# Stores of weight factors moved to GpSimd's queue, and the order of factor work on ScalarE and VectorE changed, in a fused gated cross-attention and FFN kernel

## The chip, the cores and the metric

The kernel runs on one core of a Trainium2 chip. The metric is the device time of one execution in microseconds, the median of three runs. Before the change it is 1135.29 us (1135.28 to 1135.34).

## The reference

```python
def attn(h, mem, mask):                       # h [32,128,512], mem [32,128,512]
    scores = einsum('bsd,bmd->bsm', h, mem) / sqrt(512)
    a = softmax(where(mask, scores, -1e30), -1)
    return where(any(mask), einsum('bsm,bmd->bsd', a, mem), 0)
def ffn(x, w_gate, w_up, w_down):             # 512 -> 2048 -> 512
    h = silu(x @ w_gate) * (x @ w_up)
    # of every 4 neighbours along the 2048 keep the 2 largest by magnitude
    return sparsify_2to4(h) @ w_down
x = x + tanh(g_xattn) * attn(layernorm(x), ctx, mask)
x = x + tanh(g_ffn)   * ffn(layernorm(x), w_gate, w_up, w_down)
```

There are 32 sequences of 128 rows, so 4096 rows of 512 go through the FFN. All is float32.

## The kernel before

**Two parts.** The first part, up to about 140 us, is the attention for the 32 sequences with the layernorms; it writes the sum so far to the output in HBM and keeps the transposed, normalised rows for the FFN. Then the FFN runs in 16 steps `s` (4 pairs of 512-row blocks times 4 quarters of the 2048 hidden columns), each of two units `u = 2s` and `2s + 1`.

**A unit on TensorE.** The gate and up products of a unit go by Strassen's scheme: seven products `k = 0..6`, each for two tiles `e`, each six matmuls, since a float32 value is split into a rounded high part and a low part (high times high, high times low, low times high). That makes 84 matmuls (`product`, lines 1218 to 1222). A product waits for its weight factor (`w_lo_done`, later `w_loaded`) and for PSUM to be free again: product 0 waits for `gated0` of the unit before (`h0_done`), product 2 for `copy_a0`, product 4 for `copy_a1`, product 5 for `copy_d0`. After a unit from the third on comes the down product of the step before, `down(s-1, order)` (lines 1289 to 1291): four tiles of 12 matmuls into two PSUM buffers `ps_y`, so tile `t` waits until ScalarE has copied tile `t-2` out (`copy_y`, line 704).

**Units 1 to 7 are built, 8 to 31 reloaded.** In steps 0 to 3 the seven weight factors of the next unit are made on the way: SyncE loads pieces of the raw weights (`load_w_piece`, line 252, buffer `w_raw`), ScalarE spreads them (`spread`, line 284) into `w_blk`, VectorE forms sums (`w_sum`, lines 306 to 317), ScalarE rounds the high parts (`w_high`, line 296) into `w_ring`, VectorE subtracts for the low parts (`w_low`, line 300), and SyncE stores each factor to HBM (`store_w`, line 391, 512 KB), from where later steps load it again (`load_w`, line 398). `spread` of piece 1 waits until `w_low` of factor 5 of the unit before has read the place.

**The rest of a unit.** ScalarE copies PSUM (`copy_a0`, `copy_a1`, `copy_d0`), applies silu, takes magnitudes (`absolute`, line 677), rounds the kept hidden values (`h_high`, line 684) and copies y out (`copy_y`). VectorE adds products (`add_c11`, `add_c22`, `add_c12`), multiplies gate by up (`gated0`, `gated1`, lines 955 and 961), compares magnitudes and counts (`compare`, `count_wins`), masks (`keep`, line 995) and makes low parts (`h_low`, `dn_low` for the down weights, line 1009). `x_high_at` and `x_low_at` with `x_sum` (lines 336, 341, 348 to 358) make the row factors for the next pair, one of 14 at a time; `x_stored_at` stores them.

**Order.** Each engine's instructions run in program order, which is written out by hand. SyncE's DMA queue is in order too: an issue behind a wait waits. GpSimd only does `add_y` (line 575) in the FFN: a DMA for each tile of y that adds it to the output in HBM. `y_out` has four buffers; `copy_y` waits for the addition of four tiles before.

## Time and profile before

| what | value |
|---|---|
| median of 3 runs | 1135.29 us |
| the profiled execution's own time | 1133.34 us |
| its span, first to last instruction | 1131.6 us |
| mean granted clock of TensorE | 0.992 |
| TensorE busy with matmuls | 1084.2 us, 96% |
| VectorE busy | 811.6 us, 72% |
| ScalarE busy | 621.2 us, 55% |
| GpSimd busy | 199.3 us, 18% |
| moved by DMA | 254.76 MB, mean 225 GB/s |

Times in rows are microseconds from the span's start. A row of the timeline is start, duration, engine, line, operation, output <- inputs, sizes, count, and in brackets how long the engine sat idle before it and who released it. Matmuls overlap: a row says 0.39 us, yet one starts every 0.227 us. A table of stretches gives, for each, its length, each engine's busy time with its count of instructions, the granted TensorE clock (1.00 is 2.4 GHz, 0.50 is 1.2 GHz), the DMA engines' mean busy share and GB/s.

### The profile page before, as it was taken

The page shows a single profiled execution, that of the slowest core. Times are in us where ns is not written, and L with a number is a line of the kernel's source. Part 1 is how long each engine was busy: PE and PEld are TensorE (multiplying, and loading weights), DVE is VectorE, ACT ScalarE, POOL GpSimd, SP SyncE. Part 2 cuts the span into 40 slices and gives each one's busy share as a digit, 9 for nine tenths or more (in the row PEclk, how much of TensorE's full clock was granted, in tenths as well). Part 3 has the DMA queues.
Part 4 walks back from the last instruction along what each step waited for, and adds up shares of the span by engine and source line. Part 5 has one row for each costly group of instructions (what it writes and reads, how often), then busy time and mean ns, then how long its engine had stood idle before and what let it go on. Part 6 is the DMA issues. An engine that isn't in the chain of part 4 may idle for free.

```text
span 1131.6 us, 15204 instructions
## 1 busy us (share of the span) xinstructions
PE 1084.2 (96%) x4960; PEld 881.5 (78%) x4960; DVE 811.6 (72%) x1421; ACT 621.2 (55%) x1132; POOL 199.3 (18%) x393
## 2 busy tenths in 40 slices
PE   6988898898998999999999999999999999999998
PEld 4767676686876888888888888888888888888886
DVE  6999869888696676657685757475756666575765
ACT  6989677566665454444454545455545444444552
POOL 5777400110001111111100101111111111111001
PEclk9999998999999999999999999999999999999999
DMA  7999685798887977787779777887878666767726
GB/s 267 326 336 320 216 314 194 204 262 273 271 236 219 371 219 193 191 239 216 190 228 347 211 203 204 215 250 190 227 219 282 159 152 154 197 149 199 195 32 136
DMA packets 92350, 254.76 MB, mean 225 GB/s; under 512 B 9072, under 2 KB 9072, under 8 KB 87920
## 3 DMA queue, kind: packets, MB, share of 16 engines
q1 hardware_dynamic: 74416, 221.28, 55.9%
q0 software_dynamic: 17856, 32.51, 21.1%
q8 instruction: 40, 0.66, 0.2%
q14 instruction: 38, 0.31, 0.1%
HBM read 154.14 MB, written 99.61 MB: 224 GB/s over the span
## 4 chain that ended last, share of the span: by engine, by line
PE 72%; DVE 18%; issue 4%; DMA 3%; ACT 2%; SPq 1%; DVEq 0%; POOL 0%; ACTq 0%
PE ps_a L1218 9%; PE ps_a L1220 9%; PE ps_a L1222 9%; PE ps_y L1289 9%; PE ps_y L1291 9%; PE ps_y L1290 9%; PE ps_d L1220 4%; PE ps_d L1222 4%; PE ps_d L1218 4%; PE ps_c L1218 2%; PE ps_c L1222 2%; PE ps_c L1220 2%; DVE bn L919 2%; DVE beats L969 2%; DVE bn L878 1%
## 5 line engine op out<-in xcount | busy, mean ns | idle before, releaser
L575 POOL DMA_DIRECT2D out_rows<-y_out x124 | 107.5, 868 | 874.8 <-ACT y_out L704 850.0
L1218 PE MATMUL ps_a<-xm,w_ring 128*128 128x512 f32 x512 | 201.1, 393 | 6.0 <-DVE hidden L955 3.6
L1289 PE MATMUL ps_y<-dn,h_hi 128*128 128x512 f32 x480 | 191.0, 398 | 14.0 <-ACT y_out L704 14.0
L1220 PE MATMUL ps_a<-xm,w_ring 128*128 128x512 f32 x512 | 200.5, 392 | 0.0
L1222 PE MATMUL ps_a<-xm,w_ring 128*128 128x512 f32 x512 | 200.4, 391 | 0.0
L1291 PE MATMUL ps_y<-dn,h_lo 128*128 128x512 f32 x480 | 189.1, 394 | 0.0
L1290 PE MATMUL ps_y<-dn,h_hi 128*128 128x512 f32 x480 | 188.7, 393 | 0.0
L704 ACT ACTIVATE y_out<-ps_y,ffn_gate 128x512 f32<-128x512 f32 x124 | 85.2, 687 | 150.8 <-PE ps_y L1291 150.7
L937 DVE TENSOR_TENSOR cp<-ps_c,cp 128x512 f32<-128x512 f32 x64 | 44.1, 691 | 143.0 <-PE ps_c L1222 143.0
L684 ACT ACTIVATE h_hi<-hidden 128x512 fp32r<-128x512 f32 x128 | 73.3, 625 | 102.8 <-DVE hidden L995 102.8
L1289 PEld LDWEIGHTS ps_y<-dn,h_hi 128*128 128x128 f32 x480 | 91.2, 190 | 38.0 <-ACT y_out L704 19.2
L969 DVE TENSOR_TENSOR beats<-h_abs 128x512 bf16<-128x512 f32 x186 | 117.8, 685 | 1.3 <-ACT h_abs L677 1.3
L1218 PEld LDWEIGHTS ps_a<-xm,w_ring 128*128 128x128 f32 x512 | 96.6, 189 | 28.3 <-DVE w_ring L300 4.0
L1222 PEld LDWEIGHTS ps_a<-xm,w_ring 128*128 128x128 f32 x512 | 96.7, 189 | 20.5
L1220 PEld LDWEIGHTS ps_a<-xm,w_ring 128*128 128x128 f32 x512 | 96.7, 189 | 20.2
L1291 PEld LDWEIGHTS ps_y<-dn,h_lo 128*128 128x128 f32 x480 | 91.2, 190 | 19.8
L1290 PEld LDWEIGHTS ps_y<-dn,h_hi 128*128 128x128 f32 x480 | 91.4, 190 | 19.2
L1218 PE MATMUL ps_d<-xm,w_ring 128*128 128x512 f32 x256 | 99.7, 390 | 1.2 <-ACT hidden L660 1.2
L1220 PE MATMUL ps_d<-xm,w_ring 128*128 128x512 f32 x256 | 99.6, 389 | 0.0
L1222 PE MATMUL ps_d<-xm,w_ring 128*128 128x512 f32 x256 | 99.6, 389 | 0.0
L943 DVE TENSOR_TENSOR hidden<-ps_a,hidden 128x512 f32<-128x512 f32 x64 | 43.9, 691 | 68.8 <-PE ps_a L1222 68.3
L677 ACT ACTIVATE h_abs<-hidden 128x512 f32<-128x512 f32 x124 | 74.3, 625 | 29.7 <-DVE hidden L961 29.7
(105 smaller groups left out, 1858.9 us busy)
## 6 DMA issues: line engine op xcount, KB each, us to landing
w_ring<-w_scratch SPq DMA_DIRECT2D x147, 512.0 KB, 4.3
out_rows<-y_out POOLq DMA_DIRECT2D x124, 256.0 KB, 4.2
w_scratch<-w_ring SPq DMA_DIRECT2D x56, 512.0 KB, 5.2
xm_scratch<-x_out SPq DMA_DIRECT2D x42, 512.0 KB, 5.2
xm<-xm_scratch SPq DMA_DIRECT2D x21, 1024.0 KB, 7.5
w_raw<-in_L_ffn_w_down SPq DMA_DIRECT2D x9, 1024.0 KB, 7.5
x_in<-in_x SPq DMA_DIRECT2D x32, 256.0 KB, 5.1
ctx_in<-in_ctx SPq DMA_DIRECT2D x32, 256.0 KB, 5.5
```

What stands on the lines that cost most here:

```text
L575: nc.gpsimd.dma_start(out[RING * (n // (2 * TILES * QS)) + TILES * ORDER[order] + n % TILES], y_out[:, n % 4], accum_op=ALU.add).then_inc( ...
L677: nc.scalar.activation(abs_of(s, order)[:, j], hidden[:, h, j], ACT.Abs).then_inc(abs_done, 1)
L684: nc.scalar.activation(h_hi[:, h, j], hidden[:, h, j], ACT.Copy).then_inc(h_hi_done, 1)
L704: nc.scalar.activation(y_out[:, n % 4], ps_y[n % 2][:], ACT.Identity, scale=ffn_gate[:]).then_inc(y_copied, 1)
L937: nc.vector.tensor_tensor(cp[:, e, 0], ps_c[e][:], cp[:, e, 0], ALU.add).then_inc(c11_done[e], 1)
L969: nc.vector.tensor_tensor(beats[:, PAIR[i, j]], abs_of(s, order)[:, i], abs_of(s, order)[:, j], ALU.is_ge).then_inc(beats_done, 1)
L1218: nc.tensor.matmul(to, w_ring[:, k, e, 0, c], xm[:, k, 0, c], start=begins and c == 0, stop=False, skip_group_check=not begins)
L1220: nc.tensor.matmul(to, w_ring[:, k, e, 0, c], xm[:, k, 1, c], start=False, stop=False, skip_group_check=not begins)
L1222: last = nc.tensor.matmul(to, w_ring[:, k, e, 1, c], xm[:, k, 0, c], start=False, stop=c == 1, skip_group_check=not begins)
L1289: nc.tensor.matmul(to, h_hi[:, h, j, at], right[:, 0, j], start=at_j == 0, stop=False)
L1290: nc.tensor.matmul(to, h_hi[:, h, j, at], right[:, 1, j], start=False, stop=False)
L1291: last = nc.tensor.matmul(to, h_lo[:, h, j, at], right[:, 0, j], start=False, stop=at_j == GROUP - 1)
```

## The change

It moves the stores of the factors of units 1 to 7 (49 stores of 512 KB) from SyncE's queue to GpSimd's, between the additions of y; the seven of unit 0 stay. A second set of semaphores, `w_stored_later`, counts them. On ScalarE it moves the high parts 2 to 6 of a factor set one place back among the copies of y, so that 2 and 3 stand behind the second copy and not the first; in even units it moves `w_high` of factor 1 and `spread` of piece 3 ahead of `h_high` and silu, and `spread` of piece 1 behind two magnitudes; in step 1 the first copy of y goes ahead of `h_high`; `x_high_at` goes behind the last copy. On VectorE `dn_low(0)` goes from before `add_c12(1, ·)` to behind `gated1(1, 1)`, and in odd units the low parts 4 and 5 go ahead of `keep`, 6 behind it, and `x_low_at(s, 3)` behind that.

```diff
             if u > 0:
                 act.wait_ge(made[k], 2 * u)
-                act.wait_ge(w_stored[k], 16 * u)
+                if u == 1:
+                    act.wait_ge(w_stored[k], 16)
+                else:
+                    act.wait_ge(w_stored_later[k], 16 * (u - 1))
...
             load_w_piece(sp, 2, 2)
-            for k in range(5):
-                store_w(1, k)
             load_dn(0)
-            store_w(1, 5)
+            load_w_piece(sp, 2, 3)
             x_stored_at(0, 0)
-            load_w_piece(sp, 2, 3)
-            store_w(1, 6)
             load_w_piece(sp, 3, 0)
-            store_w(2, 0)
-            store_w(2, 1)
             x_stored_at(0, 1)
             load_w_piece(sp, 3, 1)
-            for k in range(2, 6):
-                store_w(2, k)
             x_stored_at(0, 2)
-            store_w(2, 6)
             x_stored_at(0, 3)
...
-                        store_w(u + 1, 0)
-                        store_w(u + 1, 1)
                         x_stored_at(s, 2 * half + 1)
                         if half == 1:
                             load_dn(s)
-                        for k in range(2, PROD):
-                            store_w(u + 1, k)
...
+            def store_w(u, k):
+                pool.wait_ge(w_lo_done, 7 * u + k + 1)
+                nc.gpsimd.dma_start(w_dram[u, k], w_ring[:, k]...).then_inc(w_stored_later[k], 16)
+            for u in range(1, 3):
+                for k in range(PROD):
+                    store_w(u, k)
+            for s in range(1, STEPS):
+                for half in range(2):
+                    u = 2 * s + half
+                    building = u + 1 < BUILT
+                    for t in range(TILES):
+                        if building:
+                            for k in ((0, 1), (), (2,), (3,))[t]:
+                                store_w(u + 1, k)
+                        add_y(TILES * (2 * (s - 1) + half) + t)
+                    if building:
+                        for k in range(4, PROD):
+                            store_w(u + 1, k)
...
                     copy_a0(u, 1)
+                    absolute(s - 1, 1, 2)
+                    absolute(s - 1, 1, 3)
                     if building:
                         spread(act, u + 1, 1)
-                    absolute(s - 1, 1, 2)
-                    absolute(s - 1, 1, 3)
...
                         w_high(act, u + 1, 0)
                         spread(act, u + 1, 2)
+                        w_high(act, u + 1, 1)
+                        spread(act, u + 1, 3)
+                    if s == 1:
+                        copy_y(s - 1, 0, 0)
                     for j in tiles[:2]:
                         h_high(s - 1, 1, j)
                     silu1(u, 0)
                     silu1(u, 1)
-                    if building:
-                        w_high(act, u + 1, 1)
-                        spread(act, u + 1, 3)
                     for t in range(TILES):
-                        copy_y(s - 1, 0, t)
+                        if s > 1 or t > 0:
+                            copy_y(s - 1, 0, t)
                         if building:
-                            for k in ((2, 3), (4, 5), (6,), ())[t]:
+                            for k in ((), (2, 3), (4, 5), (6,))[t]:
                                 w_high(act, u + 1, k)
-                        if t == 2:
-                            x_high_at(s, 1)
+                    x_high_at(s, 1)
...
-                    dn_low(0)
                     add_c12(1, 0)
                     add_c12(1, 1)
                     w_low(dve, nc.vector, 2, 4)
...
                     gated1(1, 1)
+                    dn_low(0)
                     x_low_at(0, 2)
...
                 count_wins(s, 0)
+                if building:
+                    w_low(dve, nc.vector, u + 1, 4)
+                    w_low(dve, nc.vector, u + 1, 5)
                 keep(s, 0, kept_order(s))
+                if building:
+                    w_low(dve, nc.vector, u + 1, 6)
                 x_low_at(s, 3)
-                if building:
-                    for k in range(4, PROD):
-                        w_low(dve, nc.vector, u + 1, k)
```

The odd half on ScalarE gets the same shift of `w_high` and `x_high_at` among its copies of y.

## Rows read from the trace of the kernel before

**Rows 1.** The page: span, and the two DMA queues with their share.
```profile
span 1131.6 us, 15204 instructions
...
q1 hardware_dynamic: 74416, 221.28, 55.9%
q0 software_dynamic: 17856, 32.51, 21.1%
```

**Rows 2.** Table of stretches: the building steps, a later stretch, one within.
```profile
141.50:367.90 226.40, 205.23 (x857) 164.98 (x856) 179.82 (x294) 146.09 (x244) 17.46 (x20) 0.96 0.78 247
...
452.80:481.10 28.30, 28.30 (x126) 23.38 (x125) 19.55 (x34) 12.13 (x21) 3.46 (x4) 1.00 0.76 192
...
176.50:181.50 5.00, 5.00 (x12) 3.94 (x13) 5.00 (x9) 3.50 (x7) 0.00 (x0) 0.50 0.71 277
```

**Rows 3.** Waits of TensorE, 141.5 to 367.9 us: total, times, longest.
```profile
PE ps_y L1289 <- ACT y_out L704: 14.0, 6, 4.6
```

**Rows 4.** Timeline of TensorE: starts behind a wait, and one without.
```profile
176.48 0.77 PE L1218 MATMUL ps_a<-xm,w_ring 128*128 128x512 f32 x1 [3.62 <-DVE hidden L955]
...
209.19 0.78 PE L1289 MATMUL ps_y<-dn,h_hi 128*128 128x512 f32 x1 [4.59 <-ACT y_out L704]
...
222.63 0.39 PE L1218 MATMUL ps_a<-xm,w_ring 128*128 128x512 f32 x1
...
259.01 0.47 PE L1218 MATMUL ps_a<-xm,w_ring 128*128 128x512 f32 x1 [0.80 <-ACT cp L654]
...
274.32 0.50 PE L1289 MATMUL ps_y<-dn,h_hi 128*128 128x512 f32 x1 [1.39 <-ACT y_out L704]
...
280.22 0.50 PE L1289 MATMUL ps_y<-dn,h_hi 128*128 128x512 f32 x1 [2.89 <-ACT y_out L704]
...
327.14 0.47 PE L1218 MATMUL ps_a<-xm,w_ring 128*128 128x512 f32 x1 [1.41 <-ACT cp L654]
...
342.83 0.50 PE L1289 MATMUL ps_y<-dn,h_hi 128*128 128x512 f32 x1 [1.77 <-ACT y_out L704]
...
348.73 0.50 PE L1289 MATMUL ps_y<-dn,h_hi 128*128 128x512 f32 x1 [2.88 <-ACT y_out L704]
```

**Rows 5.** Timeline of ScalarE in the building steps.
```profile
164.96 1.12 ACT L284 ACTIVATE w_blk<-w_raw 128x512 f32<-128x512 f32 x1 [3.35 <-DMA w_raw<-in_L_ffn_w_up]
...
181.14 0.58 ACT L590 ACTIVATE cp<-ps_a 128x512 f32<-128x512 f32 x1
...
208.47 0.67 ACT L704 ACTIVATE y_out<-ps_y,ffn_gate 128x512 f32<-128x512 f32 x1
...
212.48 1.15 ACT L296 ACTIVATE w_ring<-w_blk 128x512 fp32r<-128x512 f32 x2 [3.34 <-DVE w_blk L313]
...
253.09 1.14 ACT L284 ACTIVATE w_blk<-w_raw 128x512 f32<-128x512 f32 x1 [1.73 <-issue]
...
278.44 1.15 ACT L296 ACTIVATE w_ring<-w_blk 128x512 fp32r<-128x512 f32 x2 [4.18 <-DVE w_blk L313]
```

**Rows 6.** Timeline of VectorE: first weight sum, dn's low parts, an x sum, low parts.
```profile
166.11 0.69 DVE L306 TENSOR_TENSOR w_blk<-w_blk 128x512 f32<-128x512 f32 x1 [3.78 <-ACT w_blk L284]
...
171.44 2.49 DVE L1009 TENSOR_TENSOR dn<-dn_raw,dn 128x512 fp32r<-128x512 f32 x4
...
191.09 0.69 DVE L351 TENSOR_TENSOR x_blk<-x_blk 128x512 f32<-128x512 f32 x1
...
251.72 1.89 DVE L300 TENSOR_TENSOR w_ring<-w_blk,w_ring 128x512 fp32r<-128x512 f32 x3
```

**Rows 7.** Timeline of SyncE's queue: DMA issues.
```profile
155.42 0.65 SPq L252 DMA_DIRECT2D w_raw<-in_L_ffn_w_up  x1
...
253.05 3.59 SPq L391 DMA_DIRECT2D w_scratch<-w_ring  x5
256.69 1.36 SPq L252 DMA_DIRECT2D w_raw<-in_L_ffn_w_up  x2
```

**Rows 8.** Timeline of GpSimd, and all loads of weight pieces from issue to landing.
```profile
240.16 0.86 POOL L575 DMA_DIRECT2D out_rows<-y_out  x1 [20.96 <-ACT y_out L704]
...
DMA to landing us min/median/max: 3.5/5.3/12.0
```

More of the change, by code:

```diff
@@ L225, in flamingo_gated @@
         w_stored = [sem(f"w_stored{k}") for k in range(PROD)]
+        w_stored_later = [sem(f"w_stored_later{k}") for k in range(PROD)]
         w_loaded = [sem(f"w_loaded{k}") for k in range(PROD)]
@@ L396, in load_w @@
                 if u == RELOADED[0]:
-                    sp.wait_ge(w_stored[k], 16 * BUILT)
+                    sp.wait_ge(w_stored[k], 16)
+                    sp.wait_ge(w_stored_later[k], 16 * (BUILT - 1))
                 sp.dma_start(w_ring[:, k].rearrange("p e h c m -> p (e h c m)").bitcast(F32), w_dram[weights_of(u), k]
@@ L576, in add_y @@
                                     accum_op=ALU.add).then_inc(y_stored[n % 4], 16)
-            for s in range(STEPS):
-                for t in range(TILES):
-                    add_y(2 * TILES * s + t)
-                if s != LAST:
-                    for t in range(TILES, 2 * TILES):
-                        add_y(2 * TILES * s + t)
+            def store_w(u, k):
+                pool.wait_ge(w_lo_done, 7 * u + k + 1)
+                nc.gpsimd.dma_start(w_dram[u, k], w_ring[:, k].rearrange("p e h c m -> p (e h c m)").bitcast(F32)
+                                    ).then_inc(w_stored_later[k], 16)
+            for u in range(1, 3):
[13 more added lines that the diff above has]
+                            store_w(u + 1, k)
+            for t in range(TILES):
+                add_y(2 * TILES * LAST + t)
         @block.scalar
@@ L862, in _ @@
                     if building:
-                        for k in ((2, 3), (4, 5), (6,), ())[t]:
+                        for k in ((), (2, 3), (4, 5), (6,))[t]:
                             w_high(act, u + 1, k)
-                    if t == 2:
-                        x_high_at(s, 3)
+                x_high_at(s, 3)
             for t, tiles in enumerate(((), kept_order(LAST)[:1], kept_order(LAST)[1:], ())):
```

## The prediction

> **What bounds the kernel now.** I read the page first, then the table of stretches, then TensorE's waits, then the timelines of TensorE, ScalarE, VectorE and SyncE around each wait. In the stretch from 452.8 us TensorE is busy all of the time at the full clock, 126 matmuls in 28.3 us, one every 0.225 us [rows 2]; the table looks the same from about 370 to 1100 us. Nothing that this change touches can gain there. In the building steps, 141.5 to 367.9 us, TensorE is busy 205.2 of 226.4 us at a mean clock of 0.96 [rows 2]: 21.2 us idle, and at most 0.04 x 226.4 = 9.1 us lost to the clock. So about 30 us is all that can be had, and only if everything is cured. Of the idle time 14.0 us, in six waits, is the down product waiting for a copy of y [rows 3]. The clock falls behind the longest waits: after the 3.62 us wait at 176.48 [rows 4] the stretch from 176.5 runs at 0.50, the 1.2 GHz level, 12 matmuls in 5.0 us instead of 22 [rows 2].
>
> The losses by step, each wait with what the slow clock adds behind it (its slow matmuls times 0.2 us): step 0, 3.8 + 2.6 us at 176.48 and 1.3 us in two small gaps before it; step 1, 0.5 us at 193 and 4.75 + 1.7 + 0.6 at 209.19; step 2, 0.95 at 259.01, 1.55 at 274.32, 3.05 + 1.5 at 280.22; step 3, 1.57 at 327.14, 1.93 at 342.83, 3.04 + 1.6 at 348.73 [rows 4]. Sum 30.4, which agrees with the bound above.
>
> **The change part by part.** I count in positions on the old time axis and write what each would be afterwards. VectorE starts an operation every 0.60 us, `w_sum` every 0.75, ScalarE every 0.52 (its x2 and x4 rows, as 2.49 us for four [rows 6]).
>
> **1. Stores leave SyncE's queue, step 0.** The wait at 176.48 goes back to VectorE's first sum at 166.11, which waited 3.78 us for the spread at 164.96, which had waited 3.35 us for its piece [rows 5, 6]. That piece was issued at 155.42 [rows 7], as soon as it could be, and took 9.5 us, since five stores, the down weights and more stood before it. The stores can now go as their low parts are done, up to 8 us earlier, when the DMA engines have idle time. At the median landing of 5.3 us [rows 8] it is there at 160.8; ScalarE is free at 161.6. So spread and sums come 3.35 us earlier, which also takes away the small gaps. `dn_low(0)`, four low parts or 2.4 us [rows 6], now stands behind the gating, so `gated0(1,0)` ends at 170.7 and TensorE's wait of 3.62 us disappears.
>
> Next comes what was hidden. VectorE still has the same work between 161 and 191 us and no idle time in it except these 3.8 us. `copy_a0(2,0)`, at 181.14 [rows 5], stands behind an `x_high` that needs an x sum behind `dn_low`: 176.8 + 1.1 + 0.6 gives 178.5, while TensorE would want it at 176.65: 1.95 us of wait, and 0.7 more for the second tile. Then product 5 wants `copy_d0`, which stands behind `h_high` and the x sum of 191.09 [rows 6], now 3.6 us earlier at 187.5: another 2.0 us of wait.
>
> **2. Copy of y first, step 1.** The copy at 208.47 [rows 5] stood behind two `h_high`, two silus, a high part and a spread. Now it goes ahead of them, at 197.9, so the 4.59 us wait [rows 4] is gone. The second copy ends at 204.0 against a wish of 203.2: 0.9 us left. The two high parts behind it wait for the sums: on the old axis until 212.48 [rows 5], now 208.9. Behind them on ScalarE are five high parts in all, two copies, one `x_high` and then `copy_a0(3,0)`: 208.9 + 9 x 0.52 + about 0.1 = 213.7, and product 2 of unit 3 wanted it at 212.2: 1.6 us. It then starts at 213.8 and stood at 222.63 [rows 4]. **Steps 0 and 1 give 8.8 us**: 16.1 lost before, 7.2 after. A fall of the clock behind one of the 2 us waits would cost at most 2.6 (what it cost at 176.48), but it would mostly be taken up by the next wait, because VectorE sets the pace here.
>
> **3. Steps 2 and 3.** The waits at 259.01 and 327.14 are for `copy_a1`, which was late because `spread` of piece 1 waited (1.73 us at 253.09 [rows 5]) for the low part of factor 5 among the three at 251.72 [rows 6]. Now factors 4 and 5 come before `keep`, done by 249.8, and the spread comes behind two magnitudes; `keep` ends 1.2 us later, yet `copy_a1` ends at 257.3, before TensorE needs it at 258.05. Both waits go: 0.95 and 1.57. VectorE comes 1.1 us earlier to the low parts of h. With spread and high part 1 done while ScalarE would be idle, the first copy of y ends at 271.7 for a wish of 271.6, leaving 0.2 of 1.55; in step 3 it leaves 0.9 of 1.93. The second copy no longer waits for two high parts (4.18 us idle at 278.44 [rows 5]), so the waits at 280.22 and 348.73 and the slow clock behind them, 4.55 and 4.64, go. What is late next is `copy_a0(5,0)` behind those high parts: 277.3 + 9 x 0.52 = 282.0 for a wish of 282.65, just in time. **Step 2 gives 0.95 + 1.35 + 4.55 = 6.9, step 3 gives 1.57 + 1.0 + 4.64 = 7.2 us.**
>
> **4. SyncE's issues.** In step 1 five stores stood before the pieces at 256.69 [rows 7], and these landed after 268. Now `x_low_at(s,3)` is 1.8 us later on VectorE and delays the down weights by as much, to about 254.1, but the pieces are issued at 255. If they came as late as before, ScalarE would reach the first copy at 273.4, as now, and the second would still be free: then 1.35 of this step is lost, not more.
>
> **5. GpSimd.** Forty-nine issues more. An addition takes it 0.86 us [rows 8]; a store has as many rows of twice the length, so I take 0.86, with 0.86 to 1.7 as bounds: 6 to 12 us in a half of 28. Behind a waiting store stand additions; their landing is awaited by `copy_y` a whole half later (some 25 us), with about 14 us to spare. Cost nothing; if the cover went, it would be rival C. The transfer itself: no row shows a plain store on this queue. On SyncE's queue 512 KB cost 0.559 x 1131.6 / 221.28 x 0.524 = 1.5 us of all sixteen engines; an addition of 256 KB costs 0.211 x 1131.6 / 124 = 1.93 us, so by the byte 3.85 [rows 1]. An addition also reads what it adds to, so I take 1.5 and keep 1.5 to 3.85 for rival B.
>
> The Trainium skill, DMA: Bandwidth & Descriptors, section Issuing engines are not separate DMA queues, says that all issuers share the same sixteen engines and that another issuer saves only the issuing sequencer's time. By that alone the piece of step 0 would land as late as before, 164.9, and steps 0 and 1 would gain some 3.4 us less. The trace differs in so far as the waits in order before an issue, 8 us for the first stores, are queue time too.
>
> **The sum.** 8.8 + 6.9 + 7.2 = 22.9 us. On the profiled execution 1133.34 - 22.9 = 1110.4; the median of the runs is 1.95 above that execution, so 1112.4 us.
>
> **Rivals.** A, half a gain: the pieces land late, so VectorE's chain starts where it did, and 2 us waits let the clock fall. Steps 0 and 1 give 5.4 less 2.6, steps 2 and 3 give 9 to 11 (the second copies of y hardly depend on DMA): 12 to 14 us, 1121 to 1123. For it: the DMA engines are 0.78 busy over these steps [rows 2]. Against it: moving the stores adds no bytes.
>
> B, slower: stores on the software queue cost by the byte what additions cost. 49 x 2.35 = 115 us of DMA time more, and 0.22 x 226.4 = 50 idle [rows 2]; the excess of 65 less the gain of 23 makes 42 us slower, 1177. It decides from (50 + 23) / 49 = 1.5 us more a store. For it: the price by the byte in the page. Against it: read and write in an addition explain that price.
>
> C, GpSimd's issue is slow beside VectorE: seven stores and four additions in 28.3 us leave (28.3 - 3.4) / 7 = 3.5 us a store. Above it additions and then copies of y are late; at 4.3 us a store, five times an addition's issue, five halves would each be 5 us longer: equal to the gain, 1135. Against it: the addition at 240.16 took 0.86 us with VectorE in its sums [rows 8]. The Trainium skill, SBUF — State Buffer, section SBUF: two separate sides, says that GpSimd is shut out from writing descriptors while VectorE runs a two-port mode, with 620 ns becoming 3100. By that factor C would come about; the trace does not show it for these operations.
>
> D, more: the waits left (7.2 and 1.1 us) vanish too, 1104 to 1107. Against it is VectorE's unbroken row of work.
>
> **How the numbers follow.** The forecast, a gain of 16 to 28 us (1107 to 1119), 0.72; D 0.05; A 0.13; C or any other way in which nothing comes of it 0.04; B and other slower ways 0.06. Faster by over 0.2% 0.90, within 0.2% (2.3 us, about what a measurement here can tell from no change) 0.04, slower 0.06. The range 1105 to 1123 holds the forecast, most of D and of A.
>
> **What would show it.** TensorE idle in 141 to 350 us falls from 21.2 to about 8 us; no granted clock of 0.50 near the down products; waits of the down product for y under 2.5 us in total; waits for `copy_a0` and `copy_d0` of 1.5 to 2 us each in step 1; the piece of step 0 landing by 162; GpSimd's stores about 0.9 us. The prediction is wrong if plain stores on GpSimd's queue show much longer, or if VectorE's operations grow beside them.

## The result and the profile after

The changed kernel takes 1120.86 us (median; 1118.38 to 1122.17) against 1135.28 us before: ratio 0.9872 with an interval of 0.9851 to 0.9893, a gain of 14.4 us or 1.3%. The time lies in the range that was given, but the forecast gain was 22.9 us. The profiled execution took 1122.06 us, 11.3 us less than that of before (1133.34). Against the median of before the four executions of after gained 13.1 to 16.9 us.

The page (engines: share of the span and instructions; queues: packets, MB, share of the sixteen DMA engines) and the table of stretches (busy time of TensorE, its weight loads, VectorE, ScalarE and GpSimd, then granted clock, DMA share, GB/s) of after:

```profile
span 1120.3 us, 15204 instructions
...
q1 hardware_dynamic: 67360, 195.58, 50.7%
q0 software_dynamic: 24912, 58.21, 27.5%
...
141.50:367.90 226.40, 215.23 (x933) 173.72 (x932) 190.62 (x314) 150.24 (x254) 47.35 (x73) 1.00 0.82 270
344.00:384.00 40.00, 36.68 (x159) 30.04 (x159) 24.41 (x41) 18.14 (x33) 5.10 (x7) 0.98 1.03 376
382.80:388.40 5.60, 5.60 (x13) 4.42 (x14) 5.57 (x12) 2.36 (x5) 0.00 (x0) 0.50 0.83 305
```

Beside [rows 1, 2]: 25.7 MB have gone from SyncE's queue to GpSimd's, which is 49 stores of 0.524 MB, as the change says. In the building steps TensorE idles 11.2 us instead of 21.2 and its clock is 1.00 instead of 0.96. But behind them, from 382.8 us, stands a stretch at 0.50, the 1.2 GHz level. Before, the list of TensorE's waits is empty from 355 to 1100 us. The stretch of before in which the same loads run:

```profile
361.90:395.30 33.40, 33.40 (x149) 27.61 (x148) 20.93 (x35) 14.21 (x25) 3.46 (x4) 1.00 1.03 368
```

The waits of TensorE (who waited for what: total, times, longest), after, 141.5 to 367.9 us, and its timeline at these waits and at the next one (start, length, operation, idle time and releaser):

```profile
PE ps_y L1299 <- DVE dn L1017: 3.8, 2, 2.2
PE ps_a L1228 <- ACT cp L598: 3.6, 3, 1.9
PE ps_d L1228 <- ACT hidden L668: 1.7, 1, 1.7
PE ps_y L1299 <- ACT y_out L712: 1.7, 4, 0.6
```
```profile
178.37 0.47 PE L1228 MATMUL ps_a<-xm,w_ring 128*128 128x512 f32 x1 [1.92 <-ACT cp L598]
...
189.14 0.47 PE L1228 MATMUL ps_d<-xm,w_ring 128*128 128x512 f32 x1 [1.74 <-ACT hidden L668]
...
203.58 0.50 PE L1299 MATMUL ps_y<-dn,h_hi 128*128 128x512 f32 x1 [0.32 <-ACT y_out L712]
...
213.41 0.47 PE L1228 MATMUL ps_a<-xm,w_ring 128*128 128x512 f32 x1 [1.32 <-ACT cp L598]
...
259.69 0.51 PE L1299 MATMUL ps_y<-dn,h_hi 128*128 128x512 f32 x1 [2.18 <-DVE dn L1017]
...
323.70 0.50 PE L1299 MATMUL ps_y<-dn,h_hi 128*128 128x512 f32 x1 [1.66 <-DVE dn L1017]
...
382.74 0.77 PE L1228 MATMUL ps_d<-xm,w_ring 128*128 128x512 f32 x1 [3.32 <-ACT hidden L668]
```

Waiting for a copy of y has fallen from 14.0 us [rows 3] to 1.7. Three things stand in its place: the waits of step 1 that the prediction names, two waits for the low parts of the down weights (`dn`, from VectorE), and the wait at 382.74.

To place the gain I take four marks from each kernel's timeline of TensorE: the first matmul of unit 1, and the ends of the down products of steps 0, 1 and 2 (second halves), which are the starts of units 4, 6 and 8. Times between marks, in us:

| stretch | before | after | gain | forecast |
|---|---|---|---|---|
| unit 1 to unit 4 (steps 0, 1) | 95.02 | 86.43 | 8.6 | 8.8 |
| unit 4 to unit 6 (step 2) | 67.51 | 63.90 | 3.6 | 6.9 |
| unit 6 to unit 8 (step 3) | 68.48 | 63.48 | 5.0 | 7.2 |
| unit 8 to the end | 748.4 | 754.6 | -6.2 | 0 |

With the 0.3 us by which unit 1 starts earlier, this makes the 11.3 us between the two profiled executions. That start (151.8 to 155.0 us in the traces of this study) is not touched by the change and moves between executions, so below I compare these stretches beside the medians.

### The profile page after: what moved, and what is told of

Read it like the earlier page. It is cut to its first block, busy times and chain, and to the rows that moved or that the text cites. A ratio compares the mean times of both kernels' runs of the same rounds, so it can differ in the third digit from the quotient of the medians.

```text
span 1120.3 us, 15204 instructions
## 1 busy us (share of the span) xinstructions
PE 1080.6 (96%) x4960; PEld 879.3 (78%) x4960; DVE 810.8 (72%) x1421; ACT 618.4 (55%) x1132; POOL 226.0 (20%) x442
## 4 chain that ended last, share of the span: by engine, by line
PE 71%; DVE 17%; DMA 5%; issue 4%; ACT 2%; SPq 1%; POOL 0%; DVEq 0%; ACTq 0%
PE ps_y L1299 9%; PE ps_y L1301 9%; PE ps_y L1300 9%; PE ps_a L1228 8%; PE ps_a L1230 8%; PE ps_a L1232 8%; PE ps_d L1228 4%; PE ps_d L1230 4%; PE ps_d L1232 4%; PE ps_c L1228 2%; PE ps_c L1232 2%; PE ps_c L1230 2%; DMA dn_raw<-in_L_ffn_w_down 2%; DVE bn L927 2%; DMA x_blk<-xnT_scratch 1%
## 5 line engine op out<-in xcount | busy, mean ns | idle before, releaser
L1299 PEld LDWEIGHTS ps_y<-dn,h_hi 128*128 128x128 f32 x480 | 90.1, 188 | 29.0 <-ACT y_out L712 5.9
L1228 PE MATMUL ps_d<-xm,w_ring 128*128 128x512 f32 x256 | 100.8, 394 | 5.1 <-ACT hidden L668 5.1
L1300 PEld LDWEIGHTS ps_y<-dn,h_hi 128*128 128x128 f32 x480 | 90.2, 188 | 18.7
L1230 PE MATMUL ps_d<-xm,w_ring 128*128 128x512 f32 x256 | 100.6, 393 | 0.0
L1232 PE MATMUL ps_d<-xm,w_ring 128*128 128x512 f32 x256 | 100.6, 393 | 0.0
```

Source lines behind the costliest of these rows:

```text
L1228: nc.tensor.matmul(to, w_ring[:, k, e, 0, c], xm[:, k, 0, c], start=begins and c == 0, stop=False, skip_group_check=not begins)
L1230: nc.tensor.matmul(to, w_ring[:, k, e, 0, c], xm[:, k, 1, c], start=False, stop=False, skip_group_check=not begins)
L1232: last = nc.tensor.matmul(to, w_ring[:, k, e, 1, c], xm[:, k, 0, c], start=False, stop=c == 1, skip_group_check=not begins)
L1299: nc.tensor.matmul(to, h_hi[:, h, j, at], right[:, 0, j], start=at_j == 0, stop=False)
L1300: nc.tensor.matmul(to, h_hi[:, h, j, at], right[:, 1, j], start=False, stop=False)
```

## Experiments

All times are medians; the kernel before took 1134.2 to 1134.9 us beside them. The theory at the outset: the two halves of the change (stores off SyncE, new order) each do part of the work; the losses are dn's late load and the x block's late load, both a matter of order on SyncE. The rivals: the shared DMA engines are full and no order helps, or VectorE's work is the bound whatever is loaded when. The marks of the kernels that carry the argument:

| stretch | before | after | stores only | order only | both moves | factors ahead | fewer comparisons |
|---|---|---|---|---|---|---|---|
| steps 0, 1 | 95.02 | 86.43 | 90.95 | 90.34 | 86.29 | 93.88 | 86.62 |
| step 2 | 67.51 | 63.90 | 65.93 | 68.14 | 61.99 | 66.26 | 60.75 |
| step 3 | 68.48 | 63.48 | 68.28 | 65.36 | 62.97 | 67.31 | 60.03 |
| unit 8 to end | 748.4 | 754.6 | 748.2 | 749.6 | 749.0 | 748.2 | 749.0 |

Each column is one traced execution, and the clock is not the same in each. The wait of 2.89 us in step 2 is there before and with stores only; seven matmuls run at 0.50 behind it before, none with stores only. That alone is most of the 1.6 us between these two columns in step 2. Differences below about 2 us between columns should be read with that in mind.

**Stores only.** The stores go to GpSimd as in after; ScalarE and VectorE keep the order of before. Against after, among others:

```diff
-                    if s == 1:
-                        copy_y(s - 1, 0, 0)
...
-                            for k in ((), (2, 3), (4, 5), (6,))[t]:
+                            for k in ((2, 3), (4, 5), (6,), ())[t]:
                                 w_high(act, u + 1, k)
```

> Only the stores of the factors of units 1 to 7 go to GpSimd's queue; ScalarE's and VectorE's order stays as before. Theory 1 (the copies of y are held up by ScalarE's order, the stores only feed step 0): the piece of step 0 lands by 161 instead of 164.9, the wait at 176.48 falls from 3.6 us to under 1, but the second copies of y in steps 2 and 3 still wait 2.9 us each for the sums, and the first copies still wait. Some 4 us faster, 1129 to 1132. Rival (stores on SyncE's queue hold up the whole of the building steps, and the order adds little): 10 us or more, 1125 or less, and the waits for copies of y under 6 us in total. In both the block of x rows of step 4 lands in time, since x_high keeps its place behind the third copy of y.

Measured 1129.22 us (1128.47 to 1130.84), ratio 0.9956 (0.9940 to 0.9973): 5.6 us. TensorE, 141.5 to 1100 us:

```profile
PE ps_y L1297 <- ACT y_out L712: 13.6, 5, 4.6
...
PE ps_a L1226 <- DVE hidden L963: 1.7, 1, 1.7
```

The first row is nearly the 14.0 us of [rows 3], the second is what is left of step 0's 3.62 us: the stores alone mend most of step 0 and leave the late copies of y. The time is in the range that was expected of theory 1.

**Order only.** The order of after on ScalarE and VectorE, the stores on SyncE's queue as before. Against after:

```diff
             load_w_piece(sp, 2, 2)
+            for k in range(5):
+                store_w(1, k)
             load_dn(0)
...
-            def store_w(u, k):
-                pool.wait_ge(w_lo_done, 7 * u + k + 1)
```

> Only ScalarE's and VectorE's order changes; all stores stay on SyncE's queue. Theory 1: the 2.9 us waits for the second copies of y and the slow clock behind them are gone, the wait at 209 too; the pieces of weights still land late (9 us in step 0), so the wait in step 0 stays at 1 to 2 us. Theory says 8 to 12 us faster, 1123 to 1127, with down weights for the down product late in steps 2 and 3 at least as much as in the changed kernel (waits for VectorE's low parts of the down weights of 2 us or more), since five stores and a later x store stand before them. Rival (stores are what matters): under 4 us faster, 1131 or more.

Measured 1127.82 us (1127.61 to 1129.04), ratio 0.9941 (0.9927 to 0.9956): 7.0 us, a little less than the 8 to 12 us expected. TensorE's waits here:

```profile
PE ps_y L1291 <- ACT y_out L704: 9.4, 4, 5.1
PE ps_y L1291 <- DVE dn L1009: 0.6, 1, 0.6
```

The waits for y go on, now for the first copy, which stands behind a spread whose piece is late. So the new order alone asks for pieces earlier than SyncE's queue brings them. From unit 1 to unit 8 the two halves gain 5.9 and 7.2 us, the whole change 17.2: some 4 us exist only with both. Of the waits for dn of 2 us or more that I expected here, one of 0.56 us came. In step 2 the down weights are issued 9.0 us behind unit 4, as late as in after, but they land 7.0 us after that, as before, where after takes 9.3.

**The down weights first.** In the odd units of the building steps, on SyncE:

```diff
-                        x_stored_at(s, 2 * half + 1)
                         if half == 1:
                             load_dn(s)
+                        x_stored_at(s, 2 * half + 1)
```

> The changed kernel, with SyncE's load of the down weights ahead of the x store that it stood behind in odd units of steps 1 and 2. Theory (the new waits of 2.18 and 1.66 us for low parts of the down weights come from that place in the queue, which a later x_low moved by 4 us on the clock of TensorE): the load is issued some 8 us earlier, both waits vanish, ScalarE does not wait 5.5 us before dn_high, and 4 us are gained by 370 us. If nothing else is late: 1117. Rival (DMA throughput: the engines are 1.0 busy there, and what is issued earlier only pushes the pieces of the factors back): the waits turn into waits for pieces, gain under 1.5 us. A second theory on what follows: TensorE's wait of 3.3 us at 382.7 for the block of x rows stays as it is.

Measured 1119.05 us (1117.45 to 1121.19), ratio 0.9863 (0.9848 to 0.9878), 1.8 us below after; from unit 1 to unit 8 it gains 2.0. The load is issued at 240.57 us instead of 247.26, and what is left of the waits:

```profile
260.19 0.50 PE L1299 MATMUL ps_y<-dn,h_hi 128*128 128x512 f32 x1 [0.54 <-DVE dn L1017]
...
323.67 0.50 PE L1299 MATMUL ps_y<-dn,h_hi 128*128 128x512 f32 x1 [1.15 <-DVE dn L1017]
...
382.26 0.47 PE L1228 MATMUL ps_d<-xm,w_ring 128*128 128x512 f32 x1 [2.84 <-ACT hidden L668]
```

The gain was expected to be 4 us and both waits to vanish. How much of them was the load is seen best over all kernels. The first wait is 2.18, 1.68 and 1.58 us in three that keep the load in its place (after, x block first, x high part back) and 0.54 to 0.58 us in four with it moved (this one, both moves, stores yield, low parts of dn later): 1.0 to 1.6 us of it was the late load. The second is 1.66, 1.12 and 1.11 us without the move and 1.10 to 1.15 us with it, so no part of it is shown to be the load.

**The x block first.** The load of the next pair's x block goes ahead of the seven reads of `xm_scratch`:

```diff
                     else:
+                        if half == 1 and s % QS == QS - 1 and p < PAIRS - 2:
+                            load_x_blk(sp, p + 2, 0)
                         for k in range(PROD):
```

> The changed kernel, with SyncE's load of the next block of x rows issued before the seven loads of row factors at the end of a block pair, not behind them. Theory (that block lands late because 7 MB of row factors, issued 3.7 us later against TensorE than before, are still in the DMA engines when it is issued): the wait of 3.32 us at 382.7 and the slow clock behind it, 2.9 us, vanish: 5 to 6.4 us faster than the changed kernel, 1115. Rival (the wait comes from elsewhere, for instance the row factors or down weights are late next): at most 2 us.

Measured 1116.90 us (1115.75 to 1118.65), ratio 0.9844 (0.9830 to 0.9859), 4.0 us below after. The issues, first after, then this kernel:

```profile
347.90 7.33 SPq L427 DMA_DIRECT2D xm<-xm_scratch  x7
366.27 0.58 SPq L275 DMA_DIRECT2D x_blk<-xnT_scratch  x1
```
```profile
340.99 1.89 SPq L275 DMA_DIRECT2D x_blk<-xnT_scratch  x1
```

The wait at 382.74 and the slow stretch behind it are gone, and the stretch from unit 8 takes 748.8 us, close to the 748.4 of before. The trace gives 6.3 us, the medians 4.0 where 5 to 6.4 were expected.

**Both moves.** The last two together.

> The changed kernel with both moves on SyncE's queue: down weights ahead of the x store, and the next block of x rows ahead of the row factors. Theory (the two losses are independent): 2.0 us (what the first gave up to the end of step 3) and 6 us (what the second gave behind it) add up: 8 us faster than the changed kernel, 1113 to 1115, with no wait over 2 us behind 200 us. Rival (both pull on the same DMA time): no better than the second move alone, 1117.

Measured 1115.77 us (1114.79 to 1116.34), ratio 0.9834 (0.9821 to 0.9848): 5.1 us below after and 18.9 below the kernel before beside it. The theory expected 8 us. The marks do give 8.3 (2.6 before unit 8 and 5.7 behind it), but the executions start unit 1 at different times, and the profiled execution of after was slower than its median. Its waits (155 to 1080 us) and the row that says why dn is still late:

```profile
PE ps_a L1228 <- ACT cp L598: 3.6, 3, 1.9
PE ps_y L1299 <- ACT y_out L712: 2.2, 4, 0.6
PE ps_y L1299 <- DVE dn L1017: 1.7, 2, 1.1
```
```profile
257.36 2.48 DVE L1017 TENSOR_TENSOR dn<-dn_raw,dn 128x512 fp32r<-128x512 f32 x4
```

VectorE is busy without a break from about 236 us up to this row, so here it is its work that is late, not the transfer.

**The x high part back in its place.** Rival to the order on SyncE: the x store, and with it all that stands behind it, begins late because `x_high_at` was moved behind the last copy.

```diff
-                    x_high_at(s, 1)
+                        if t == 0:
+                            x_high_at(s, 1)
```

> The changed kernel with ScalarE's x_high of even units ahead of the second copy of y instead of behind the last one. Theory (the block of x rows of step 4 is late because the last x store of the block pair was moved back 6 us against TensorE and its landing lets the loads of row factors start): VectorE's x_low comes 2.5 us earlier in step 3 (337.6 for 340.15), the loads of row factors start 2.5 us earlier, and TensorE's wait of 3.32 us falls to about 1 us, without the slow clock: 4 to 5 us faster than the changed kernel, 1116. Rival (the amount of DMA work decides, the start does not): the wait stays at 3 us.

Measured 1119.07 us (1118.74 to 1123.87), ratio 0.9874 (0.9857 to 0.9892), 1.8 below after. The wait was expected to fall to 1 us. The reads now begin 2.3 us earlier, at 345.61, but TensorE too reaches unit 8 earlier, by 0.9 us, and the x block's load is issued with it. What is left is a wait of 2.54 us, which the list counts with another one:

```profile
345.61 8.76 SPq L427 DMA_DIRECT2D xm<-xm_scratch  x7
365.41 0.58 SPq L275 DMA_DIRECT2D x_blk<-xnT_scratch  x1
```
```profile
PE ps_d L1229 <- ACT hidden L668: 3.3, 2, 2.5
```

Against TensorE the reads begin only 1.4 us sooner than in after, and the wait is 0.8 us shorter. That does not clear the late start. All kernels traced with the x block behind the seven reads, in us (lead: from the first read's issue to the start of unit 8; chain: from that issue to ScalarE's first use of the x block):

| kernel | lead | chain | wait of TensorE |
|---|---|---|---|
| stores only | 24.2 | 35.3 | 0 |
| before | 21.3 | 33.4 | 0 |
| order only | 20.7 | 34.0 | 0.85 |
| x high part back | 19.2 | 34.2 | 2.54 |
| down weights first | 17.9 | 33.3 | 2.84 |
| after | 17.7 | 33.6 | 3.32 |

The less the lead, the longer the wait, while the chain hardly changes: the DMA engines are full in it, with a share of 1.03 before and after.

**Stores yield.** Both moves, and GpSimd's stores of factors 2 to 6 wait in odd units until the down weights and the next pieces have landed:

```diff
+                        if half == 1:
+                            pool.wait_ge(dn_raw_loaded, 16 * (s + 1))
+                            pool.wait_ge(w_raw_loaded[1], 16 * (2 * (u + 2) + 2))
```

> The kernel with both moves, and GpSimd's stores of factors 2 to 6 in odd units of steps 1 and 2 held until the down weights and the next pieces have landed. Theory (DMA bandwidth, not the place in the queue, is what is left: 2.6 MB of stores run between 240 and 255 us beside the down weights and the pieces): ScalarE's waits for pieces (17.8 us in four with the down weights first) fall by half or more, TensorE's waits of about 1 us for the low parts of the down weights go, 1.5 to 3 us faster than the kernel with both moves. Rival (the sixteen engines are taken by the additions of y, not by the stores): no change within 0.7 us.

Measured 1115.46 us (1114.78 to 1117.13), ratio 0.9835 (0.9821 to 0.9848): no difference from both moves. ScalarE's waits for pieces (230 to 345 us) did fall, from the first row (both moves) to the second (stores yield):

```profile
ACT w_blk L285 <- DMA w_raw<-in_L_ffn_w_up: 15.8, 4, 4.9
```
```profile
ACT w_blk L285 <- DMA w_raw<-in_L_ffn_w_up: 8.5, 2, 4.3
```

Halving them brought TensorE nothing: unit 8 starts 211.25 us behind unit 1 in both. My theory that stores crowd out loads that TensorE then needs has fallen for these two steps.

This trace shows one thing more. The same wait of 1.92 us as in after is followed here by seven matmuls at the 1.2 GHz level, one every 0.43 us (a duration of 0.63 marks them in the rows):

```profile
181.41 0.47 PE L1231 MATMUL ps_a<-xm,w_ring 128*128 128x512 f32 x1 [1.92 <-ACT cp L601]
...
182.72 0.63 PE L1233 MATMUL ps_a<-xm,w_ring 128*128 128x512 f32 x1
...
192.18 0.47 PE L1231 MATMUL ps_d<-xm,w_ring 128*128 128x512 f32 x1 [0.75 <-ACT hidden L671]
```

The next wait is 0.75 us instead of 1.74, and steps 0 and 1 take 86.46 us against 86.29 with both moves.

**Low parts of dn later in step 1.**

```diff
                         h_low(0, 0, j)
+                    dn_low(0)
                     compare(0, 1, first + second)
...
                     gated1(1, 1)
-                    dn_low(0)
```

> The kernel with both moves, and VectorE's four low parts of the first down weights moved further back, from behind gated1(1,1) to behind the first low parts of h in step 1. Theory (VectorE's unbroken work sets the pace from 161 to 212 us, and its place in that work decides which copy is late): the x sum that copy_a0(2,0) stands behind, and the one before product 5, come 2.4 us earlier; the waits at 178 (1.92 us) and 189 (1.74 us) go, and the 1.3 us wait before product 2 of unit 3 grows in part; 1 to 2 us faster than the kernel with both moves. Rival (it only moves the waits): the down product waits for the low parts by as much, no change within 0.5 us.

Measured 1115.48 us (1113.98 to 1116.04), ratio 0.9831 (0.9817 to 0.9844), within 0.5 us of both moves as the rival had it. The wait at 178 is gone and one of 2.36 us at 192.5 has come; unit 8 again starts 211.25 us behind unit 1. Here VectorE's order only chooses where TensorE waits.

**Fewer comparisons.** Both moves, with the six comparisons of each second half in steps 1 and 2 on a quarter of their columns. That leaves out part of the choice of the two largest of four; the kernel only measures what VectorE's work costs.

```diff
+                    at = slice(0, HALF // 4 if order == 1 and s in (1, 2) else HALF)
```

> The kernel with both moves on SyncE's queue; VectorE's six comparisons of the second halves of steps 1 and 2 run on a quarter of the columns (the other three quarters keep old results, so the masks of these halves are not the reference's). Theory (in steps 2 and 3 TensorE now waits for VectorE's unbroken row of work, not for a transfer): some 0.4 us less in each of six comparisons puts the low parts of the down weights 2.4 us earlier; TensorE's waits for them (0.57 and 1.11 us) go, and those for copies of y at 266 and 329 (0.6 us each) too: 2 to 3 us faster than the kernel with both moves, 1113. Rival (a transfer ends last there): no change within 0.7 us.

Measured 1111.57 us (1109.82 to 1112.17), ratio 0.9793 (0.9776 to 0.9810): 4.2 us below both moves; between the marks 3.85 us are gained before unit 8. All waits for dn are gone from the list, in which `ACT cp L598` with 3.5 us is now the largest. No slow stretch falls into these steps here or with both moves. So in steps 2 and 3 VectorE's work is what ends last; less of it gives 1.2 and 2.9 us.

**Factors ahead of the second copy.** Both moves, with the old tuple `((2, 3), (4, 5), (6,), ())` in both loops over the copies of y.

> The kernel with both moves, with the high parts 2 to 6 of the factors back in their old place, one copy of y earlier. Theory (this shift is the largest single term): the second copies of y wait for the weight sums again, TensorE 2.9 us each in steps 2 and 3 with 1.5 us of slow clock behind, and in step 1 where the slack is smaller 4 us or more; 10 to 13 us slower than the kernel with both moves, 1126 to 1129. Rival (with the stores off SyncE's queue the sums are in time): under 3 us slower.

Measured 1131.47 us (1131.36 to 1133.28), ratio 0.9977 (0.9967 to 0.9988): 15.7 us slower than both moves, where 10 to 13 were expected. Steps 2 and 3 lose 4.3 us each and steps 0 and 1 lose 7.6, where 4 or more were expected.

```profile
PE ps_y L1299 <- ACT y_out L712: 16.4, 4, 6.9
```

**Copy late.** Both moves, with step 1's first copy of y behind the silus again, and high part 1 and the spread of piece 3 behind them too.

```diff
-                    if s == 1:
-                        copy_y(s - 1, 0, 0)
...
                     silu1(u, 1)
+                    if building:
+                        w_high(act, u + 1, 1)
+                        spread(act, u + 1, 3)
```

> The kernel with both moves, with ScalarE's high part of factor 1, spread of piece 3 and first copy of y in step 1 back behind h_high and silu. Theory: in step 1 the first copy is late by some 5 us again, of which about 3 are taken up by the waits that follow; in steps 2 and 3 the first copies are late by 1 to 1.5 us more than now: 5 to 7 us slower, 1121 to 1123. Rival (the sums of the weights, and with them VectorE, gain nothing from the early spread, and the copy in step 1 is all): 2 to 3 us slower.

Measured 1118.79 us (1118.37 to 1120.53), ratio 0.9865 (0.9850 to 0.9880): 3.0 us slower by the medians, 4.9 by the traces from unit 1 to the end. The theory expected 5 to 7 and the rival 2 to 3, so this run does not decide between them. Most of the loss in the trace, 4.4 us, lies in steps 0 and 1; the wait in step 1 is back at 4.59 us, as in [rows 4].

**Stores on SyncE in a good order.** Both moves, but all 49 stores on SyncE's queue, set where they hold up no load:

```diff
+            for k in range(3):
+                store_w(1, k)
             load_w_piece(sp, 2, 2)
+            for k in range(3, 5):
+                store_w(1, k)
             load_dn(0)
...
                         load_w_piece(sp, u + 1, 2)
                         load_w_piece(sp, u + 1, 3)
+                        if u > 2:
+                            for k in range(2, PROD):
+                                store_w(u, k)
```

> All stores stay on SyncE's queue, with the changed order on ScalarE and VectorE and both moves of the kernel before it, but factors 2 to 6 are stored behind the next unit's first two pieces and the down weights instead of ahead of them, and in step 0 three stores go ahead of the piece that they stood behind. Theory (what counts is that loads do not stand behind stores that wait or fill the DMA engines, and GpSimd's queue is only one way to it): within 2 us of the kernel with both moves, 1115 to 1118. Rival (only a second queue gets the loads out in time): 1120 or more, with waits for pieces as with the order alone.

Measured 1116.80 us (1114.72 to 1119.36), ratio 0.9845 (0.9822 to 0.9869). Unit 8 starts 211.25 us behind unit 1, as with the stores on GpSimd. Step by step the two differ: step 2 takes 64.04 us here against 61.99, step 3 60.96 against 62.97, and behind unit 8 there is a wait of 1.5 us for the down weights' low parts. Within the noise of the medians, then, the second queue is one way to the gain and a good order on the first is another.

## Why the prediction was right in part

**Part 1, stores off SyncE (right).** The piece of step 0 was issued at 153.75 us and there when ScalarE was free for it: its spread starts at 161.19 without a wait (forecast 161.6; before 164.96 behind 3.35 us, [rows 5]).

```profile
161.19 1.13 ACT L285 ACTIVATE w_blk<-w_raw 128x512 f32<-128x512 f32 x1
```

The rule of the Trainium skill that I set against this (DMA: Bandwidth & Descriptors, section Issuing engines are not separate DMA queues: another issuer saves issuing time alone) gave 3.4 us less for steps 0 and 1; the trace gives 8.6 of the 8.8 us without that cut. The stores on SyncE in a good order bear the rule out in another sense: by the medians GpSimd's queue as such brought nothing that the order before each issue did not bring too.

**Part 2, copy of y first (right, also in its positions).** The prediction put the starts behind a wait at 178.5, 204.1 and 213.8; they stand at 178.37, 203.58 and 213.41. The waits are 1.92, 0.32 and 1.32 us for 1.95, 0.9 and 1.6; the wait for `copy_d0` is 1.74 for 2.0. In this execution none of them let the clock fall. Where it did fall behind the first of them, in the traces of x high part back, stores yield and stores on SyncE, steps 0 and 1 took 86.00 to 86.46 us, no longer than with both moves (86.29). So the sentence that a fall of the clock "would mostly be taken up by the next wait, because VectorE sets the pace here" is borne out. Moving VectorE's order (low parts of dn later) points the same way.

The 16.1 us lost before in these steps is right, though the prediction's own list gives only 15.25. The stretch of 95.02 us holds 348 matmuls, and at one every 0.2267 us they take 78.9.

**Part 3, steps 2 and 3: a term mis-sized, 3.3 and 2.2 us.** The second copies were right: the old tuple costs 4.3 us in each of the two steps, for 4.55 and 4.64 forecast. The failed step is "`keep` ends 1.2 us later, yet `copy_a1` ends at 257.3", and with it part 4's "1.8 us later on VectorE": the prediction has no term for a wait of TensorE for VectorE's low parts of the down weights. Such waits came, 2.18 and 1.66 us. I counted these steps on the old distance between VectorE and TensorE. But step 1 had just used it up: it gave TensorE 8.6 us, and VectorE had no idle time to give back. `keep` of step 1's second half, before and after:

```profile
248.70 0.69 DVE L995 SCALAR_TENSOR_TENSOR hidden<-part,hidden 128x512 f32<-128x512 bf16 x1
```
```profile
242.91 0.69 DVE L1003 SCALAR_TENSOR_TENSOR hidden<-part,hidden 128x512 f32<-128x512 bf16 x1
```

The unit before it began at 247.15 and 238.25 us, so `keep` stands 1.55 us behind TensorE before and 4.66 after, 3.1 us later where I took 1.2. With less of VectorE's work these waits go, and 3.85 us come back between the marks (fewer comparisons). That VectorE is late there, and what its lateness costs, is measured; that step 1 is where the slack went is read from the marks and not tried by itself.

**Part 4, SyncE's issues (a step not followed to its end).** It says that the down weights load later by 1.8 us and stops. The load was issued 5.3 us behind the start of unit 4 before and 9.0 after (at 247.26 us), so 3.7 us later, and it took 9.3 us to land instead of 7.0. That second part comes with the stores on GpSimd's queue: the landing takes 7.0 us in the two kernels with the stores of before on SyncE's queue and 8.4 us with stores only. Letting some of the stores wait (stores yield, 8.6) did not bring it back, so which transfers stand in its way stays open. ScalarE, which makes dn's high parts first, stood 5.54 us for it; VectorE's `dn_low` and TensorE's 2.18 us stand behind:

```profile
256.48 2.19 ACT L702 ACTIVATE dn<-dn_raw 128x512 fp32r<-128x512 f32 x4 [5.54 <-DMA dn_raw<-in_L_ffn_w_down]
```

Loading them first takes 1.0 to 1.6 us off that wait and nothing that is shown off step 3's. So the 3.3 us missed in step 2 are in part this load (the step takes 62.29 and 61.99 us with it moved, for 63.90) and in part VectorE's work (1.2 us more). In step 3 VectorE's work is all that the runs show.

**"Nothing that this change touches can gain there" (a loss left out, 6.2 us, the largest miss).** A stretch in which TensorE is never idle can't gain, but it can lose, and I put no price on that. The next pair's x block, after and before:

```profile
366.27 0.58 SPq L275 DMA_DIRECT2D x_blk<-xnT_scratch  x1
...
381.48 0.63 ACT L340 ACTIVATE x_out<-x_blk 128x512 fp32r<-128x512 f32 x1 [6.87 <-DMA x_blk<-xnT_scratch]
```
```profile
383.78 0.57 SPq L274 DMA_DIRECT2D x_blk<-xnT_scratch  x1
...
395.30 0.63 ACT L336 ACTIVATE x_out<-x_blk 128x512 fp32r<-128x512 f32 x1 [3.18 <-DMA x_blk<-xnT_scratch]
```

TensorE reaches unit 8 17.5 us earlier, at 365.63 instead of 383.14. The x block is issued 0.6 us behind that point in both, but lands at 381.5 instead of 395.3, only 13.8 earlier: 3.7 us late against TensorE. ScalarE stands 6.87 us for it with `copy_d0` behind, TensorE waits 3.32 us, and the 14 matmuls at the slow clock behind it take 2.9 us more than at the full one. Why the landing gained less: the seven reads of row factors before it begin at 347.90 us instead of 361.87, only 14.0 us earlier, and from there to the x block's landing the engines are full in both kernels (share 1.03) and take 33.6 us after, 33.4 before. The reads wait until the last x store has landed. It was issued 1.1 us ahead of unit 7 before (352.08) and 5.2 us behind its start after (340.87). With `x_high_at` moved back it is 2.7 us behind, so that move makes 2.5 us of it; the rest I put down to VectorE's work being late against TensorE, which no run shows by itself.

Putting the x block ahead of the seven reads cures it (4.0 us by the medians). Moving `x_high_at` back gives 1.4 us of lead and shortens the wait by 0.8. A full cure by starting the reads earlier was not tried, nor whether stores that GpSimd issues up to 345.3 us add to the crowd.

**Part 5, GpSimd (right, and too careful).** All 49 stores, each with its time to issue in ns (shortest, median, longest), and their way from issue to landing:

```profile
L572 POOL DMA_DIRECT2D w_scratch<-w_ring x49: 531/533/901, 140.9 to 345.3; - x49
...
DMA to landing us min/median/max: 2.9/5.4/8.2
```

A store issues in 0.53 us where I took 0.86 to 1.7, so rival C had nothing to stand on. The shut-out that the Trainium skill describes (SBUF — State Buffer, section SBUF: two separate sides, 620 ns becoming 3100) does not appear: the longest is 901 ns with VectorE busy 84% of the stretch, and the stores land as soon after their issue as SyncE's did (median 5.4 us, before 5.2). No trace here says whether any of VectorE's operations ran in that mode, so this is no test of the rule itself. The additions went from 868 to 889 ns on average.

Rival B had the price of a store between 1.5 and 3.85 us of all sixteen engines. GpSimd's queue rose by 0.275 x 1120.3 - 0.211 x 1131.6 = 69.3 us for 49 stores, 1.41 us each; SyncE's fell by 0.559 x 1131.6 - 0.507 x 1120.3 = 64.6, 1.32 each. B is refuted; the price is even a little under the lower bound of 1.5.

**Rival A** named 1121 to 1123 us, which is near the result, by another mechanism. It had the pieces late and the clock low in the building steps. The piece was early there and the granted clock is 1.00; the loss came later. That the measured time lies nearer to A than to the forecast is no proof of A.

**The median.** I added 1.95 us between the profiled execution and the median of before. For after the median is 1.2 us below its profiled execution. That swing of 3.1 us is why the medians show 14.4 us and the traces 11.3. The mean granted clock of the four executions of after is 0.995 to 0.998 and only one was traced, so how the loss is split in the others is not known.

## What to carry to other kernels

Give a busy stretch a price on the side of loss: when a change makes the bottleneck engine reach a point 17 us earlier, list every load whose chain of transfers does not start as much earlier, and compare its landing with the new demand. Advance the distance between two engines from stage to stage; slack that an earlier stage has used up can't be counted again. On a queue that works in order, ask what stands before the load that is due: moving the stores to another issuer and setting them behind the loads gave the same time within the noise.

The best version tried is the change with both moves on SyncE, 1115.77 us: 19 us or 1.7% below before, with every computation left in.

## What the runs showed of the hardware

- The granted clock fell to 0.50 for 5.6 us behind the wait of 3.32 us at 382.74 in after. Waits of 1.92, 2.18 and (in the kernel that loads the down weights first) 2.84 us were followed by no such stretch there.
- The length of a wait does not decide it alone. The same wait of 1.92 us in step 1 left the clock at 1.00 in after and with both moves; in the traces of x high part back, stores yield and stores on SyncE it (1.91 or 1.92 us) was followed by seven or eight matmuls at the 1.2 GHz level. The wait of 2.89 us in step 2 was followed by seven such matmuls before and by none with stores only.
- A plain store of 512 KB takes GpSimd 0.53 us to issue, an addition of 256 KB 0.89. In time of the sixteen engines, worked out from the queues' shares of the two pages, the store takes 1.41 us on this queue and 1.32 on SyncE's, an addition of half the bytes 1.93.
